# The first batch's maxima moved ahead of the second batch's parts, and six steps of a serial chain moved from the prologue to the MLP

## The reference, cut to what matters

```python
ada = silu(c) @ W_ada + b_ada                 # six groups of 144: shift, scale, gate, twice
h = layernorm(x) * (1 + scale_msa) + shift_msa
q, k, v = split(h @ W_qkv + b_qkv)            # 16 heads of 9
attn = softmax(q * 9 ** -0.5 @ k.T)
x = x + gate_msa * (attn @ v @ W_proj + b_proj)
h = layernorm(x) * (1 + scale_mlp) + shift_mlp
x = x + gate_mlp * (gelu(h @ W_fc1 + b_fc1) @ W_fc2 + b_fc2)
U, _ = qr(P)                                  # P is 144 x 64
R = expm(A(silu(c) @ W_rot.T + b_rot))        # one antisymmetric 64 x 64 matrix a batch
x = x + (x @ U @ R - x @ U) @ U.T
```

## Time and profile before

| | us |
|---|---|
| three timed executions | 372.08, 375.44, 376.39 |
| their median | 375.44 |
| the profiled execution, its own time | 375.6 |
| its span, first to last instruction | 373.5 |

### The profile page before, as it was taken

The page is one execution under the profiler, slowest core; times in us unless marked ns, Lnnn a source line. Parts: engine busy times, 40 slices in busy tenths (PEclk is TensorE's granted clock), DMA queues, the critical chain, the costliest instruction groups (busy, mean ns, idle before and its releaser), DMA issues.

```text
span 373.5 us, 7750 instructions
## 1 busy us (share of the span) xinstructions
PE 299.3 (80%) x2717; PEld 185.7 (50%) x2717; DVE 244.9 (66%) x762; ACT 145.8 (39%) x270; POOL 120.6 (32%) x307
## 2 busy tenths in 40 slices
PE   2888966887977769698889887989578998896684
PEld 1333523444434335365555555566546676665563
DVE  6757567667768868979889798753514445554443
ACT  2111112487575634645556464644103323330000
POOL 5812804205208293244271432122350333300000
PEclk9999999999999996999999999999758999997555
DMA  3923321121712312212123000000000000000004
GB/s 117 280 69 105 84 64 28 49 78 41 198 46 54 92 41 57 73 30 67 55 49 86 14 3 4 4 2 0 3 1 0 2 0 2 1 2 0 0 2 126
DMA packets 20285, 18.00 MB, mean 48 GB/s; under 512 B 3541, under 2 KB 18087, under 8 KB 20122
## 3 DMA queue, kind: packets, MB, share of 16 engines
q1 hardware_dynamic: 19638, 16.38, 16.4%
q10 hardware_dynamic: 610, 1.14, 1.1%
HBM read 12.32 MB, written 4.81 MB: 46 GB/s over the span
## 4 chain that ended last, share of the span: by engine, by line
PE 53%; DVE 29%; issue 7%; SPq 4%; ACT 3%; POOL 2%; DMA 1%; DVEq 0%; POOLq 0%; ACTq 0%
DVE nm L930 12%; PE m L651 6%; PE pst L629 5%; PE m L485 5%; PE ps L451 5%; PE pst L265 4%; DVE gp L737 3%; PE m L287 3%; PE m L271 3%; PE pst L382 3%; PE pst L472 2%; DVE gm L738 2%; PE pst L266 2%; SPq L255 2%; PE m L265 2%
## 5 line engine op out<-in xcount | busy, mean ns | idle before, releaser
L930 DVE TENSOR_REDUCE nm<-ps 128x2 f32<-128x512 f32 x128 | 87.7, 689 | 33.3 <-PE ps L451 29.2
L1164 ACT ACTIVATE pex<-pst 128x1024 f32<-128x1024 f32 x64 | 65.6, 1025 | 27.8 <-PE pst L472 27.0
L451 PE MATMUL ps<-ks,qs 54*128 54x256 bf16 x256 | 28.2, 296 | 25.9 <-DVE nm L930 25.3
L767 DVE TENSOR_SCALAR pm<-m 64x1 f32<-64x1 f32 x64 | 13.6, 213 | 47.1 <-PE m L287 46.5
L485 PE MATMUL m<-pex,ve 128*32 128x256 f32 x512 | 35.7, 398 | 0.0
L1484 POOL TENSOR_TENSOR xin<-xin,res 128x288 f32<-128x288 f32 x16 | 12.7, 794 | 70.9 <-DVE res L959 70.9
L287 PE MATMUL m<-qst,ident 64*64 64x64 f32 (+42 forms) x128 | 20.3, 238 | 13.0 <-DVE qst L773 13.0
L451 PEld LDWEIGHTS ps<-ks,qs 54*128 54x128 bf16 x256 | 10.5, 97 | 39.9 <-issue 35.3
L472 PE MATMUL pst<-qs,ks 56*128 56x256 bf16 x256 | 26.5, 284 | 3.9 <-DMA qs<-nmT 3.1
L271 PE MATMUL m<-gm,ident 64*64 64x65 f32 x126 | 23.8, 276 | 7.0 <-DVE gm L738 3.9
L651 PE MATMUL m<-wfc,gT 128*128 128x144 f32 x160 | 27.1, 324 | 0.0
(11 more groups left out here) (253 smaller groups left out, 571.0 us busy)
## 6 DMA issues: line engine op xcount, KB each, us to landing
scr_qk<-parts SPq DMA_DIRECT2D x24, 144.0 KB, 2.0
qs<-scr_qk SPq DMA_DIRECT2D x96, 36.0 KB
ks<-scr_qk SPq DMA_DIRECT2D x72, 36.0 KB
gates<-scr_ada SPq DMA_DIRECT2D x2, 576.0 KB, 6.5
out_dram<-xin SPq DMA_DIRECT2D x8, 144.0 KB, 2.0
wr<-in_L_cond_W_dram SPq DMA_DIRECT2D x1, 1134.0 KB
xin<-in_x_dram SPq DMA_DIRECT2D x1, 864.0 KB, 5.3
ks<-scr_qk ACTq DMA_DIRECT2D x24, 36.0 KB
```

The costliest lines, as they stand in the source:

```text
L451: ins = mm(ps[e][:, L * i:L * i + L], qs[64 * e:64 * e + KS, b % 3, 2 * g + i, 128 * lt:128 * lt + 128], ks[64 * e:64 * e + KS, b % 3, 2 * ...
L930: nc.vector.tensor_reduce(nm[:, lt, e, 2 * g:2 * g + 2], ps[e][:, :].rearrange("p (h l) -> p h l", h=2), AX.X, ALU.max, negate=True).then_ ...
L1164: nc.scalar.activation(pex[:, n % 4, :, :], pst[0][:, :, :], ACT.Exp, scale=ATT_SCALE).then_inc(s("exp_done"), 1)
```

## The change

- `PROLOGUE_STEPS` goes from 14 to 8 and `TAIL_STEPS` from 6 to 7. The number of steps in the attention turns stays, but each is six places earlier in the chain. The MLP has 57 steps now: 7 for each of the batches 0 to 7 and one in the last round.
- In the MLP the seventh step stands at the end of a batch: on PE behind `transpose_h`, on DVE behind `gated("fc2", t)`.
- In the prologue the first batch's q and k are projected in one go at k = 2, and the second batch is transposed right behind them. The second batch's q and k follow at k = 3, 4 and 5, the modulation's rests at k = 6. DVE takes the first batch's parts and the second's last channels at k = 2, and the statistics of the other batches at k = 4 to 7.
- DVE's rests and parts of the second batch move into the opening turn, behind the maxima of chunks 0, 1 and 2.
- The values of batch 0 are split over chunks 0 and 1 in the opening turn; those of batch 1 move to chunk 2 of turn 0. The second piece of the rotation weights moves from chunk 1 to chunk 0 of turn 0.
- ACT issues the first batch's k stack, takes both high parts of the second batch, and only then copies the modulation's rests and re-orders the stacked weights; the wait for these weights moves from the start of the turns to the third batch's projection.
- POOL zeroes `ve` behind the second batch's normalisation.

```diff
@@ -42,10 +42,10 @@
     K_RUNS = [(5, 0, 1, 1), (3, 0, 2, 1), (0, 0, 3, 1)]
 
 
-    PROLOGUE_STEPS = 14
+    PROLOGUE_STEPS = 8
     N_BASIS = 6
     CHAIN = (R - 1) + N_BASIS + R
-    TAIL_STEPS = 6
+    TAIL_STEPS = 7
 
     ctx = ExitStack()
     with ctx:
@@ -244,7 +244,7 @@
                 SQUARES[t, n] = len(SQUARES)
         assert len(SQUARES) == SQUARINGS
 
-        TURNED = [(0, 7), (1, 6), (2, 5), (3, 5), (4, 5), (6, 5), (7, 5), (7, 6)]
+        TURNED = [(0, 7), (0, 5), (2, 5), (3, 5), (4, 5), (6, 5), (7, 5), (7, 6)]
 
         def stack_rows(eng, b, to, which, row, part, n, repeat):
 
@@ -417,6 +417,8 @@
                     claim(pe, bank, name, b)
                     if b < 2:
                         pe.wait_ge(s("hTf_ready"), b + 1)
+                    elif b == 2:
+                        pe.wait_ge(s("wqk_stacked"), 4)
                 m = shared[bank]
                 for c in chunks:
                     cols = slice(QC * c, QC * c + QC)
@@ -427,15 +429,16 @@
                 if part in (None, 1):
                     filled(last, name, b)
 
-            def values(b, bank):
-                m = claim(pe, bank, "values", b)
-                for lt in range(LT):
+            def values(b, bank, halves=range(LT)):
+                m = claim(pe, bank, "values", b) if 0 in halves else shared[bank]
+                for lt in halves:
                     rows = slice(128 * lt, 128 * lt + 128)
                     if b < 2:
                         last = project(m[:, C * lt:C * lt + C], hTa[:, b % 2, rows], hTf[:, b, rows], wqkv_a[:, 2 * C:3 * C], wqkv_b[:, 2 * C:3 * C])
                         continue
                     last = project(m[:, C * lt:C * lt + C], hTa[:, b % 2, rows], hTr[:, b % 2, rows], wqkv_a[:, 2 * C:3 * C], wqkv_r[:, 2 * C:3 * C])
-                filled(last, "values", b)
+                if LT - 1 in halves:
+                    filled(last, "values", b)
 
             def maxima(b, n):
 
@@ -520,12 +523,12 @@
                         maxima(t + 1, n)
                     chain(chain_steps(t, n))
                     if t == -1:
-                        if n == 0:
-                            values(0, 6)
-                        if n == 1:
-                            values(1, 7)
+                        if n < LT:
+                            values(0, 6, (n,))
                         if n == 4:
                             shift(0, 0, 5)
+                    if t == 0 and n == 2:
+                        values(1, 6)
                     if n == 0 and real(t - 1):
                         weighted(t - 1, G - 1, 7)
                     if n == 1:
@@ -591,25 +594,20 @@
                 if k == 2:
                     modulation_columns()
                     transpose_h(0, 6)
-                if k == 3:
                     pe.wait_ge(s("wqk_ready"), 8)
                     qk("qk2", (2,), 0, 7)
+                    qk("qk01", (0, 1), 0, 5)
+                    transpose_h(1, 6)
+                if k == 3:
+                    qk("qk2", (2,), 1, 7)
                 if k == 4:
-                    qk("qk01", (0,), 0, 5, 0)
+                    qk("qk01", (0,), 1, 5, 0)
+                if k == 5:
+                    qk("qk01", (1,), 1, 5, 1)
                 if k == 6:
-                    qk("qk01", (1,), 0, 5, 1)
-                    transpose_h(1, 6)
-                if k == 7:
                     modulation_rests()
-                if k == 8:
-                    qk("qk2", (2,), 1, 7)
-                if k == 10:
-                    qk("qk01", (0,), 1, 5, 0)
-                if k == 12:
-                    qk("qk01", (1,), 1, 5, 1)
             pe.wait_ge(s("ones_ready"), 4)
             pe.wait_ge(s("identb_ready"), 1)
-            pe.wait_ge(s("wqk_stacked"), 4)
             pe.wait_ge(s("hTf_ready"), 2)
             pe.wait_ge(s("pT_ready"), 1)
             for t in range(-1, B):
@@ -712,6 +710,8 @@
                     chain(mlp_steps(t, 5))
                 if t >= 0 and real(t + 2):
                     transpose_h(B + t + 2, 5)
+                if t >= 0:
+                    chain(mlp_steps(t, 6))
             for i in range(3):
                 rotate_basis(i, 5 + i)
             pe.wait_ge(s("fq_ready"), 3)
@@ -980,6 +980,13 @@
                             generator()
                     if n == 2 and real(t - 1):
                         by_token(t - 1, 1)
+                    if t == -1:
+                        if n == 0:
+                            rest_of("qk2", 1, 2, 1)
+                        if n == 1:
+                            rest_of("qk01", 1, 0, 2)
+                        if n == 2:
+                            split(1)
                     if n == 3:
                         if t == -1:
                             shift(0, 0)
@@ -1016,24 +1023,18 @@
                     modulation_columns()
                     last_channels(0)
                     statistics(range(2, 4), "mv_ready")
-                if k == 3:
-                    batch_rows()
-                if k == 4:
-                    rest_of("qk2", 0, 2, 1)
                     dve.wait_ge(s("pT_filled"), 1)
                     nc.vector.tensor_copy(pT[:, :], ps[0][0:R, 0:C]).then_inc(s("pT_ready"), 1)
-                if k == 6:
+                    rest_of("qk2", 0, 2, 1)
                     rest_of("qk01", 0, 0, 2)
                     split(0)
                     last_channels(1)
-                if 7 <= k < 11:
-                    if k == 7:
+                if k == 3:
+                    batch_rows()
+                if 4 <= k < 8:
+                    if k == 4:
                         dve.wait_ge(s("x1_loaded"), 16)
-                    statistics(range(4 + 3 * (k - 7), 7 + 3 * (k - 7)), "mv_ready")
-                if k == 10:
-                    rest_of("qk2", 1, 2, 1)
-            rest_of("qk01", 1, 0, 2)
-            split(1)
+                    statistics(range(4 + 3 * (k - 4), 7 + 3 * (k - 4)), "mv_ready")
             for t in range(-1, B):
                 turn_a(t)
 
@@ -1187,14 +1189,14 @@
                     if real(t):
                         exp(t, n)
                     if t == -1:
-                        if n == 0:
+                        if n == 1:
                             evac_values(0)
-                        if n == 1:
-                            evac_values(1)
                         if n == 2:
                             stack_of_k(1)
                         if n == 4:
                             shift(0, 0)
+                    if t == 0 and n == 2:
+                        evac_values(1)
                     if n == 0 and real(t - 1):
                         evac_oT(t - 1, G - 1)
                     if n == 1:
@@ -1226,13 +1228,13 @@
             high_part("qk2", 0, 2, 1)
             high_part("qk01", 0, 0, 2)
             evac_hT(1)
+            stack_of_k(0)
+            high_part("qk2", 1, 2, 1)
+            high_part("qk01", 1, 0, 2)
             act.wait_ge(s("msr_filled"), 1)
             nc.scalar.copy(msr[:, :, :, :].rearrange("p b i c -> p (b i c)"), st_bank[0][:, :]).then_inc(s("msr_ready"), 1)
-            stack_of_k(0)
-            high_part("qk2", 1, 2, 1)
             act.wait_ge(s("wstack_loaded"), 7 * 16)
             by_dimension(wqk_r, wqkv_r, "wqk_stacked")
-            high_part("qk01", 1, 0, 2)
             for t in range(-1, B):
                 turn_a(t)
 
@@ -1505,9 +1507,6 @@
                 nc.gpsimd.memset(one_more[:, 2 * i, :], 0.0)
                 nc.gpsimd.memset(one_more[:, 2 * i + 1, :], 1.0).then_inc(s("one_more_ready"), 1)
             nc.gpsimd.memset(hTf, 1.0).then_inc(s("hTf_one"), 1)
-            nc.gpsimd.memset(ve[:, :, :, :, :], 0.0).then_inc(s("ve_zeroed"), 1)
-            pool.wait_ge(s("ve_zeroed"), 1)
-            nc.gpsimd.memset(ve[:, :, :, :, D:D + 1], 1.0).then_inc(s("ve_zeroed"), 1)
             nc.gpsimd.memset(onesb[:, :], 1.0).then_inc(s("ones_ready"), 1)
             nc.gpsimd.memset(otok[:, :, C:C + 1], 1.0).then_inc(s("ones_ready"), 1)
             nc.gpsimd.memset(hr[:, :, :, 6 * CB:SR], 1.0).then_inc(s("ones_ready"), 1)
@@ -1524,6 +1523,9 @@
             pool.wait_ge(s("mv_ready"), 2)
             deviations(slice(2, 4))
             normalise(1)
+            nc.gpsimd.memset(ve[:, :, :, :, :], 0.0).then_inc(s("ve_zeroed"), 1)
+            pool.wait_ge(s("ve_zeroed"), 1)
+            nc.gpsimd.memset(ve[:, :, :, :, D:D + 1], 1.0).then_inc(s("ve_zeroed"), 1)
             pool.wait_ge(s("mv_ready"), 6)
             deviations(slice(4, NT))
             normalise(2)
```

## The result

The changed kernel takes 392.87 us (median of 4, 388.93 to 396.75) against 373.76 for the kernel before (median of 4). The medians are 19.1 us apart. The forecast was 390.2, in a range of 378 to 398. The profiled execution took 396.75, with a span of 394.7, against 375.6 and 373.5; its time is the longest of the four.

A forecast was written before the change was run, and what follows sets the result against it. PE and DVE, handing work to and fro, were taken to bound the kernel. From the profiled 375.6 us, minus 4.9, plus 1.3, 8.4 and 10.0 gave 390.4, or 390.2 against the median; whole range 378 to 398.

The forecast's parts named there:

- prologue and opening turn: Before turn 0: six fewer chain steps and the second batch's work moved bring turn 0 forward, 4.9 us gained.
- turn 0: First attention turn: the second batch's values added in chunk 2 cost 1.3 us, between 0 and 3.1.
- turns 1 to 7: Attention turns: eight steps each as before, elimination steps replacing sign steps; no change, give or take 1 us.
- MLP, serial gap: Changes of batch in the MLP: step 0 directly follows step 6, delaying the up projection; 8.4 us lost, bounds 7 and 10.
- MLP, the clock: MLP: the new gaps make PE's clock fall, 4.0 us each time; 10.0 us lost.
- the number of falls: Five changes of batch in the MLP: between 0 and 5 clock falls, the middle taken, 2.5.
- The rival built on it: MLP: only the serial gap costs and the clock stands the five gaps; 380.4 us, chance 0.23.
- POOL's brake: Opening turn: POOL's third batch's last part, ready at 45.4, holds back the fifth maxima until 46.3 instead of 51.19.
- The memset: Prologue, POOL: filling `ve`, 2.9 us, falls from idle time into idle time, at no cost or gain.
- the second rival: Opening turn and turn 0: PE's clock climbs early, 3 us saved, no falls in the MLP; 377.4 us, chance 0.08.

The follow-up runs named there:

- experiment 2: Changed kernel with six chain steps moved from the MLP into the last attention turn, six a batch in the MLP; 382.5 us, ratio 1.023 to the kernel before.
- experiment 3: Changed kernel with a chain step placed within the up projection's second half, so none of the seven are back to back; 377.9 us, ratio 1.013 to the kernel before.
- experiment 4: Changed kernel with unread float32 products on PE filling the two waits at each change of batch; 381.8 us, ratio 1.024 to the kernel before.
- experiment 5: Kernel before with only POOL's zeroing of `ve`, its wait and small memset moved behind the second batch's normalisation; 372.48 us against 373.19, ratio 0.997.
- Experiment 6: Experiment 3's kernel with the second batch's values back in the opening turn, one half each in chunks 2 and 3; 373.7 us, ratio 0.997 to the kernel before.
- Experiment 1: Kernel before with only seven chain steps a batch in the MLP instead of six, prologue kept at 14 steps; 387.9 us, ratio 1.038.
- experiment 8: Kernel before with unread products on PE in its own long waits at the MLP's start and in the last rounds; 365.4 us, ratio 0.981.

## Why the prediction was right, point by point

| term | predicted | measured in the profiled execution |
|---|---|---|
| prologue and opening turn | -4.9 | -6.6, of it about -2.3 an earlier start of DVE beside POOL's memsets |
| turn 0 | +1.3 | +1.0; +2.8 to +4.3 in experiments 2 to 4 |
| turns 1 to 7 | 0 | +3.9 |
| MLP, serial gap | +8.4 | +7.6 (experiment 4) |
| MLP, the clock | +10.0 | +15.3 (changed kernel less experiment 4), of it 1.9 ahead of the first fall |
| sum | +14.8 | +21.2 |

The path, the two neighbouring steps and the falling clock, was right. That the forecast of 390.2 lies 2.7 us from the median of 392.87 is in part luck: the number of falls was the middle of a wide guess, the term for the prologue was 1.7 us short of the gain, two losses were too small or missing, and against the execution whose terms are in the table the sum misses by 6.4 us.

**The serial gap** held as laid out: the wait of 1.35 us behind the gated product, five times, and an up projection later by 1.6. Experiment 4's MLP is 132.2 us from the last exponential on, the kernel before has 124.6. Batch 1's stretch at 1.2 GHz is also shorter in experiment 4, so 7.6 is a low end for this term: against experiment 2, whose clock is as high there (10.24 us), experiment 4's second column is 1.75 us longer, and against the kernel before only 0.55.

**The clock** was the right mechanism and mis-sized: 2.5 falls of 4.0 us each were put in. Four came, and together they cost 13.5 us, 3.4 on average but 1.5 for the first: a price taken from one low stretch of 17 us doesn't hold for stretches of 3.4 to 13.7. That the gaps cause the falls was an argument from one case before; experiment 4 shows it, since it changes nothing but what fills them. Which gap makes the clock fall can't be read off a stretch's busy time: the emptiest of the five didn't. This may be why the time varies, 387.8 to 399.3 over all executions: the mean granted clock was 0.858 at 396.75 and 0.912 at 388.93, but 0.873 at 390.63, and with a single trace of this kernel it is not shown. The Trainium skill's rule ("TensorE: Matmul & The Clock Gate", "Why this matters for your kernels"), by which only longer idle gaps than these lower the clock, doesn't agree with four falls where PE's longest wait was 1.35 us. The rival built on it, 380.4, is what the kernel takes when the gaps are filled (381.8).

**The prologue's gain** was 4.4 us against experiment 5 (59.48 to 55.13), 0.5 less than laid out: POOL's brake was where it was put, but ACT, still issuing k transfers, kept the third batch's first q and k waiting for 1.69 us, a wait that the kernel before doesn't have there. The memset was costed at nothing because POOL was idle on both sides. That looked at the engine that moved and not at the one beside it: DVE's first operation, held up until 6.08 in the profiled execution before, ends at 3.73 in the changed kernel. How often it is held up is open, so 2.3 us is what these two executions differ by, and not a steady price.

**Turn 0** was within its bounds in the profiled execution and at or over their upper end in three others with the same turn 0 (32.2, 33.7 and 32.3 us against 29.4). In the profiled one the clock climbed early, at about 54, as the second rival had it, but fell at 57.2 and gave nothing lasting. Experiment 6 shows the term to be the values' move.

**Turns 1 to 7** were costed at nothing and lost 3.9 us, 0.8 in turn 3 and 2.4 in turn 6. The clock was at 0.50 there for 3.4 us from 152.8 and for 6.8 us from 214.2; the kernel before has neither of these two. Experiment 1, with the old attention turns, has a fall at 156.2 too; experiment 3 has one in turn 6, experiments 2, 4 and 6 have none. Turn 6 took 23.3 us in both executions with that fall and 20.6 in the three without it, against 20.9 before, so that fall is the 2.4 us. Whether the basis steps, now in turn 6, make it likelier there is open.

## What to carry to other kernels

A serial chain that is strewn through other work costs nothing only while each of its steps has other work of at least one trip's length behind it; before adding a step, find two neighbours with nothing between them, on the engine that works in order. The same gap costs twice where it lets TensorE's clock fall, so compare a new wait with the stretches at which the clock already fell, and expect falls at some of such places and not at others (at four of five here). Before a gain of 1 to 3 us in a trace is put down to an edit, look whether another execution with the same code up to there has it too. And where a wait can't go, products that nobody reads may pay: here they took 2% off the kernel before.

## What the runs showed of the hardware that was not expected

- A DVE operation on 8 partitions took 3.31 and 3.51 us beside a POOL memset of 2.65 us over 128x3072, with which it ended; it took 0.22 us when it ran ahead of POOL's next memsets (experiments 5 and 8), and about 1.1 beside the short ones that the changed kernel leaves there.
- PE's clock can be held by idle work: in experiment 4 a filled gap of 1.35 us left it at 2.4 GHz over 71.3 us, and in experiment 8 the rotated basis' 24 products took 1.69 us instead of 3.15.
- The granted clock reads 1.00 up to the first recorded fall even where PE runs at 1.2 GHz; in the changed kernel the maxima's four products go from 0.61 us at 50.96 to 0.39 at 54.07 with no change in the clock row.
